# Mix features of two heads taken together, on alternating row halves of the array

## The reference, cut to what matters

```python
q = (hidden_states @ Wq.T).reshape(b, s, H, HD)
k = (hidden_states @ Wk.T).reshape(b, s, H, HD)
v = (hidden_states @ Wv.T).reshape(b, s, H, HD)
qf = jax.nn.elu(q @ Wf.T) + 1.0
kf = jax.nn.elu(k @ Wf.T) + 1.0
kv = jnp.einsum('bshf,bshd->bhfd', kf, v)
out = jnp.einsum('bshf,bhfd->bshd', qf, kv)
k_sum = kf.sum(axis=1)
norm = jnp.einsum('bshf,bhf->bsh', qf, k_sum)[..., None] + 1e-06
out = (out / norm).reshape(b, s, D)
```

## Time and profile before

| | |
|---|---|
| median of three runs | 1080.4 us |
| the profiled execution | 1081.49 us, its span 1079.7 us |
| mean granted TensorE clock | 0.978 |
| TensorE busy | 1024.7 us, 95% |
| VectorE, ScalarE, GpSimd busy | 793.2, 637.3, 133.2 us |
| mix stage on TensorE | from 74.75 us to about 222 us |

### The profile page before, as it was taken

How to read it: one execution, slowest core, us unless ns; L and a number is a source line. 1 busy time by engine, 2 the same in 40 slices (tenths; PEclk the granted TensorE clock), 3 DMA queues, 4 the chain that set the end, 5 groups by cost and what they waited for, 6 DMA issues and landing times.

```text
span 1079.7 us, 15085 instructions
## 1 busy us (share of the span) xinstructions
PE 1024.7 (95%) x5227; PEld 878.8 (81%) x5227; DVE 793.2 (73%) x1094; ACT 637.3 (59%) x825; POOL 133.2 (12%) x185
## 2 busy tenths in 40 slices
PE   3999999999999999988989899999999999999988
PEld 3899999998788899877778787777888878787766
DVE  6347878774677868767674588888887888788687
ACT  3257776722321133577774457777777777778582
POOL 2002223230010002132211020000000000000013
PEclk9999999999999999989899899999999999999989
DMA  8652413245646664311103279999999999999986
GB/s 283 181 176 59 117 60 113 64 124 171 176 122 201 186 192 122 115 39 39 40 1 109 92 287 366 381 353 384 385 387 344 376 387 363 372 358 388 332 308 237
DMA packets 140508, 237.33 MB, mean 220 GB/s; under 512 B 6908, under 2 KB 48124, under 8 KB 137892
## 3 DMA queue, kind: packets, MB, share of 16 engines
q1 hardware_dynamic: 135780, 225.91, 61.3%
q0 software_dynamic: 1760, 6.37, 1.5%
q10 hardware_dynamic: 2912, 4.34, 1.1%
HBM read 206.56 MB, written 30.03 MB: 219 GB/s over the span
## 4 chain that ended last, share of the span: by engine, by line
PE 68%; DVE 11%; ACT 7%; issue 5%; DMA 5%; POOL 2%; SPq 1%; ACTq 0%; DVEq 0%; POOLq 0%
PE bank L1297 28%; PE bank L962 5%; PE bank L964 5%; PE bank L963 5%; DMA raw<-in_wffn 5%; PE bank L976 4%; PE bank L978 4%; PE bank L977 4%; DVE wlo L1371 2%; PE bank L1096 2%; DVE dense L1634 1%; PE bank L1284 1%; ACT a_all L860 1%; PE bank L1179 1%; PE bank L1038 1%
## 5 line engine op out<-in xcount | busy, mean ns | idle before, releaser
L1671 DVE TENSOR_TENSOR wlo<-raw,whi 128x2048 fp32r<-128x2048 f32 x72 | 164.6, 2289 | 27.9 <-ACT whi L860 27.6
L860 ACT ACTIVATE a_all<-raw 128x2048 fp32r<-128x2048 f32 x72 | 138.1, 1917 | 53.2 <-DMA raw<-in_wffn 31.7
L860 ACT ACTIVATE whi<-raw 128x2048 fp32r<-128x2048 f32 x72 | 138.0, 1917 | 44.7 <-DMA raw<-in_wffn 23.0
L1371 DVE TENSOR_TENSOR wlo<-raw,whi 128x1024 fp32r<-128x1024 f32 (+1 forms) x72 | 120.5, 1678 | 46.6 <-ACT whi L652 45.8
L652 ACT ACTIVATE whi<-raw 128x1024 fp32r<-128x1024 f32 (+1 forms) x72 | 89.0, 1241 | 97.6 <-PE bank L964 47.7
L1671 DVE TENSOR_TENSOR t_all<-raw,a_all 128x2048 fp32r<-128x2048 f32 x36 | 82.5, 2293 | 39.2 <-ACT a_all L860 38.9
L962 PE MATMUL bank<-a_all,whi 128*128 128x384 f32 x320 | 109.3, 341 | 0.0
L964 PE MATMUL bank<-a_all,wlo 128*128 128x384 f32 x320 | 107.9, 337 | 0.0
L963 PE MATMUL bank<-a_all,whi 128*128 128x384 f32 x320 | 107.6, 336 | 0.0
L1297 PE MATMUL bank<-a_all,xg 128*128 128x512 f32 x360 | 106.8, 411 | 0.0
L1297 PE MATMUL bank<-whi,t_all 128*128 128x512 f32 x288 | 100.3, 410 | 0.0
(11 more groups left out here) (277 smaller groups left out, 2112.7 us busy)
## 6 DMA issues: line engine op xcount, KB each, us to landing
raw<-in_wffn SPq DMA_DIRECT2D x144, 512.0 KB
raw<-in_wffn SPq DMA_DIRECT2D x72, 1024.0 KB
raw<-in_wall SPq DMA_DIRECT2D x28, 1024.0 KB
raw<-in_wall SPq DMA_DIRECT2D x32, 512.0 KB
yrows<-zero SPq DMA_DIRECT2D x24, 512.0 KB, 7.0
y_rows<-zero SPq DMA_DIRECT2D x8, 1024.0 KB, 8.6
dense<-yrows SPq DMA_DIRECT2D x8, 512.0 KB, 7.7
y_rows<-dense ACTq DMA_DIRECT2D x16, 256.0 KB, 5.4
```

What stands on the lines that cost most here:

```text
L860: act.activation(hi_ring[u % RAW], raw[:, u % RAW, :], ACT.Copy).then_inc(hi_done, 2)
L1371: dve.tensor_tensor(ring(wlo, k), part(k), ring(whi, k).bitcast(F32), ALU.subtract).then_inc(lo_done, width(k))
L1671: dve.tensor_tensor(lo_ring[u % RAW], raw[:, u % RAW, :], hi_ring[u % RAW].bitcast(F32), ALU.subtract)\
```

## The change

The two heads of a chunk are taken together. In an even step the K features of heads h and h + 1 are made, in an odd step the kv of both heads, and then the Q features of both. Their matmuls alternate: head 0 of the chunk on the rows 0 to 63, head 1 on the rows 64 to 127, into different banks. The mixes of both heads stand in the next even step, one ahead of the piece and one behind it. The kv of odd heads gets its own columns of bank 0 (kv_bank). The numbers of matmuls and of operations on the other engines stay as they are.

```diff
@@ -382,12 +382,17 @@
 
         def feature(h, i):
 
+            g, part_ = i % 2, i // 2
             b = gp_bank("feat", 4 * h + i)
-            if i < 2:
-                return qf[h % 2][:, i, :], b[:, 0:N]
-            if i == 2:
-                return kf[h % 2][:, 0:2, :], b[:, :].rearrange("p (t f) -> p t f", t=2)
-            return kf[h % 2][:, 2, :], b[:, 0:FD]
+            if h % 2:
+                return qf[g][:, part_, :], b[:, 0:N]
+            if part_ == 0:
+                return kf[g][:, 0:2, :], b[:, :].rearrange("p (t f) -> p t f", t=2)
+            return kf[g][:, 2, :], b[:, 0:FD]
+
+        def kv_bank(g):
+
+            return bank[0][:, 2 * P * (g % 2):2 * P * (g % 2) + 2 * (HD + 1)]
 
         block = ctx.enter_context(nc.Block())
...
-                b = bank[0][:, 0:2 * (HD + 1)].rearrange("p (f d) -> p f d", f=2)
-                act.wait_ge(kv_full, g + 1)
+                b = kv_bank(g).rearrange("p (f d) -> p f d", f=2)
+                act.wait_ge(kv_full, g // 2 * 2 + 2)
...
 
-                if h >= 2:
-
+                if h >= 2 and h % 2 == 0:
+                    act.wait_ge(kv_full, h)
+                elif h >= 3:
                     act.wait_ge(qf_lo, h - 1)
-                    act.wait_ge(kv_full, h - 1)
...
-                act.wait_ge(feat_done, 4 * h + 2)
-                if h >= 2:
-                    act.wait_ge(mix_full, h - 1)
-                act.activation(qf_s[h % 2][:, 0, :, :], qf[h % 2], ACT.Copy).then_inc(qf_hi, 1)
+                if h % 2:
+                    act.wait_ge(feat_done, h + 1)
+                    if h >= 3:
+                        act.wait_ge(mix_full, h - 1)
+                    for g in range(2):
...
-                if 1 <= h <= H:
+                if h % 2 and h < H:
                     kv_high(h - 1)
+                    kv_high(h)
...
+            def mix(g):
+
+                pe.wait_ge(kv_ready, g + 1)
+                if g >= 1:
...
             for h in range(H + 2):
                 k = PAIRS + 2 + h
-                if h >= 2:
-                    g = h - 2
...
+                if h >= 2 and h % 2 == 0:
+                    mix(h - 2)
...
-                if 1 <= h <= H:
-                    g = h - 1
-                    pe.wait_ge(feat_done, 4 * g + 4)
-                    if g >= 1:
...
+                if h >= 2 and h % 2 == 0:
+                    mix(h - 1)
+                if h % 2 and h < H:
+                    pe.wait_ge(feat_done, h)
+                    if h >= 3:
+                        pe.wait_ge(kv_ready, h - 1)
+                    for g in (h - 1, h):
+                        for f in range(2):
+                            for t in range(NT):
+                                last = pe.matmul(kv_bank(g)[:, f * (HD + 1):(f + 1) * (HD + 1)], kf[g % 2][:, t, f * P:(f + 1) * P],
+                                                 v_tok[:, t, g, :], start=(t == 0), stop=(t == NT - 1))
+                        last.then_inc(kv_full, 1)
...
                 if h < H:
-                    for i in range(4):
-                        gp_take(pe, "feat", 4 * h + i)
...
-                            if i < 2:
-                                last = pe.matmul(b[:, 0:N], w[:, w_part, i * P:(i + 1) * P], q[:, x_part, :], start=(n == 0), stop=(n == 2))
-                        for t in range(0, 2) if i == 2 else range(2, 3) if i == 3 else ():
+                    for i in (0, 2):
+                        b = []
+                        for g in range(2):
+                            gp_take(pe, "feat", 4 * h + i + g)
+                            b.append(gp_bank("feat", 4 * h + i + g))
+                        rows_ = [slice(0, HD), slice(HD, P)]
+                        if h % 2:
+                            f = slice(i // 2 * P, i // 2 * P + P)
                             for n, (x_part, w_part) in enumerate(((0, 0), (0, 1), (1, 0))):
-                                last = pe.matmul(b[:, (t % 2) * FD:(t % 2 + 1) * FD], kk[:, x_part, t * P:(t + 1) * P],
-                                                 w[:, w_part, :], start=(n == 0), stop=(n == 2))
-                        last.then_inc(gp_full, 1)
+                                for g in range(2):
+                                    last = pe.matmul(b[g][:, 0:N], wf_s[rows_[g], w_part, f], qk[h // 2 % 2][rows_[g], 0, x_part, :],
+                                                     start=(n == 0), stop=(n == 2))
+                                    if n == 2:
+                                        last.then_inc(gp_full, 1)
+                        else:
+                            for t in range(0, 2) if i == 0 else range(2, 3):
+                                for n, (x_part, w_part) in enumerate(((0, 0), (0, 1), (1, 0))):
+                                    for g in range(2):
+                                        last = pe.matmul(b[g][:, (t % 2) * FD:(t % 2 + 1) * FD], qk[h // 2 % 2][rows_[g], 1, x_part, t * P:(t + 1) * P],
+                                                         wf_s[rows_[g], w_part, :], start=(n == 0), stop=(n == 2))
+                                        if n == 2 and t > 0:
+                                            last.then_inc(gp_full, 1)
...
+                if h >= 2 and h % 2 == 0:
+                    mix_out(h - 2)
...
+                if h >= 2 and h % 2 == 0:
+                    mix_out(h - 1)
+                for g in (h - 1, h) if h % 2 and h < H else ():
...
+                    b = kv_bank(g).rearrange("p (f d) -> p f d", f=2)
+                    dve.wait_ge(kv_hi, h + 1)
...
-                        if i == 1 or i == 3:
+                        if i == 3:
                             dve.wait_ge(gp_dve, gp_by[:gp["feat", 4 * h + i] + 1].count("dve"))
-                            dve.sem_inc(feat_done, 2)
+                            dve.sem_inc(feat_done, 1)
```

More of the change, by code:

```diff
@@ L1027, in _ @@
             pe.wait_ge(bo_added, 1)
+            def mix(g):
+                pe.wait_ge(kv_ready, g + 1)
+                if g >= 1:
+                    pe.wait_ge(mix_done, g)
+                pe.wait_ge(qf_lo, g + 1)
+                for n, (kv_part, q_part) in enumerate(((0, 0), (0, 1), (1, 0))):
+                    for f in range(2):
+                        last = pe.matmul(bank[1][:, 0:N], kv[g % 2][:, kv_part, f, :], qf_s[g % 2][:, q_part, f, :],
+                                         start=(n == 0 and f == 0), stop=(n == 2 and f == 1))
+                last.then_inc(mix_full, 1)
             for h in range(H + 2):
                 k = PAIRS + 2 + h
-                if h >= 2:
-                    g = h - 2
-                    pe.wait_ge(kv_ready, g + 1)
-                    if g >= 1:
[L1034 to L1040, removed]
+                if h >= 2 and h % 2 == 0:
+                    mix(h - 2)
                 if k < T_V:
@@ L1451, in _, with mix_out @@
             qk_low(0, 1)
+            def mix_out(g):
+                own, other = (slice(HD * (p % 2), HD * (p % 2) + HD) for p in (g, g + 1))
+                o = bank[1]
+                dve.wait_ge(mix_full, g + 1)
+                if g >= 4:
+                    dve.wait_ge(mix_norm, (g - 4) // 2 + 1)
+                dve.tensor_scalar(norm[own, g // 2 % 2, :], o[other, 0:N], 1e-6, None, ALU.add).then_inc(norm_ready, 1)
+                dve.tensor_copy(moT[own, g // 2, :], o[own, 0:N]).then_inc(mix_done, 1)
             def invert(c, half):
@@ L1463, in _ @@
                     lo(n)
-                if h >= 2:
-                    g = h - 2
-                    own, other = (slice(HD * (p % 2), HD * (p % 2) + HD) for p in (g, g + 1))
-                    o = bank[1]
-                    dve.wait_ge(mix_full, g + 1)
-                    if g >= 4:
-                        dve.wait_ge(mix_norm, (g - 4) // 2 + 1)
-                    dve.tensor_scalar(norm[own, g // 2 % 2, :], o[other, 0:N], 1e-6, None, ALU.add).then_inc(norm_ready, 1)
-                    dve.tensor_copy(moT[own, g // 2, :], o[own, 0:N]).then_inc(mix_done, 1)
+                if h >= 2 and h % 2 == 0:
+                    mix_out(h - 2)
                 if k < T_V:
                     qk_low(h // 2 + 1, h % 2)
-                if 1 <= h <= H:
-                    g = h - 1
+                if h >= 2 and h % 2 == 0:
+                    mix_out(h - 1)
+                for g in (h - 1, h) if h % 2 and h < H else ():
                     own, other = (slice(HD * (p % 2), HD * (p % 2) + HD) for p in (g, g + 1))
-                    b = bank[0][:, 0:2 * (HD + 1)].rearrange("p (f d) -> p f d", f=2)
-                    dve.wait_ge(kv_hi, g + 1)
+                    b = kv_bank(g).rearrange("p (f d) -> p f d", f=2)
+                    dve.wait_ge(kv_hi, h + 1)
                     dve.tensor_tensor(kv[g % 2][:, 1, :, own], b[:, :, 0:HD], kv[g % 2][:, 0, :, own].bitcast(F32), ALU.subtract)
```

7 lines of the change are left out of this document (2 added, 5 removed).

## The result

The changed kernel takes 1128.1 us (median of 4 runs, 1126.24 to 1131.53) against 1077.5 us for the kernel before (4 runs): the ratio is 1.047, with a 95% interval of 1.0415 to 1.0523, so it is slower by 4.7%. The prediction was 1141 us, in a range of 1120 to 1162. The direction and the mechanism came as predicted; one term of the sum, the pitch of the alternating matmuls, was mis-sized, and the drain was priced rightly for a reason that doesn't hold.

A forecast was written before the change was run, and what follows sets the result against it. TensorE was taken to bound the kernel, so new waits ahead of the mixes count in full: 1081.5 us + 44 (stage) + 16 (low clock) = 1141.5, forecast as 1141 us, range 1120 to 1162.

The forecast's parts named there:

- the sum: Whole kernel: 1081.5 us plus 44 for the longer mix stage plus 16 for the low clock, 1141.5.
- the pitch of the alternating matmuls: Q and K features on TensorE: one start every 0.114 us for both shapes, a floor taken from the kv matmuls.
- the drain: TensorE changing between 128-row and 64-row matmuls: none seen, priced at nothing; at most 5 us in all.
- What bounds the stage: Mix stage: TensorE, busy 73.41 of 74 us, so a microsecond of new wait is a microsecond of span.
- The chain from the Q features to the mix: Odd step into next mix: 7.35 us from first Relu through ScalarE, VectorE and GpSimd, with TensorE waiting eight times.
- rival 2: Q and K features: the row halves overlap fully, stage +37 us before the clock, 1134 us; chance 0.20.
- The clock: TensorE behind each of eight waits: granted clock falls, losing 2.2 us each, less 1.6 already paid; +16 us.
- The cover of the K features: Even step: K chain of about 6.0 us hidden by 2.05 + 4.16 of TensorE work; 1.1 late at the first pair.
- The other side: Mix stage: overlap hides the second half's matmuls and the mix does not wait, 1062 us; chance 0.02 for faster.

The follow-up runs named there:

- The filled wait: Changed kernel plus 60 TensorE matmuls that nobody reads, behind the Q features of each odd step; 1117.4 us, 1.038 of the kernel before.
- The kernel with the other orders: Changed kernel with mixes one step later, VectorE reading the first mix sooner, ScalarE splitting weights before copies, last mix behind last piece; 1058.9 us, 0.983.
- the later mix alone: Changed kernel with only its mixes moved one step later, behind the piece and behind the kv of odd steps; 1079.7 us, 1.0047 of the kernel before.

## Why the prediction was right, and where it was wrong

- **What bounds the stage: right.** TensorE had no slack, so a new wait in its order was paid in full, less only what the overlap saved.
- **The chain from the Q features to the mix: right**, 7.40 us for 7.35, eight waits, in the predicted place, and nothing later gave the time back. Copying one head earlier took 1.0 us off each wait.
- **The pitch of the alternating matmuls: wrong.** "I take 0.114 for both shapes" rested on the kv matmuls, which use all 128 rows and follow one another. That floor does not hold across two halves: eighteen K matmuls took 1.25 us to the next start, 0.069 each. In the single starts two partners begin 0.003 us apart, and the pairs follow at 0.11 to 0.12 us, as single matmuls did before. The first Relu starts 0.89 us behind the first Q matmul (156.11 less 155.22), 1.02 with a pitch of 0.114. This is rival 2, full overlap, +37 in place of +44 before the clock. The rule of the Trainium skill ("TensorE: Matmul & The Clock Gate", Part 3, "Measured speedup vs the span model"), that distinct row groups run concurrently, agrees: two halves gain 1.8 times (twice 1.14 us for nine matmuls, over 1.25). The prediction had set it below a floor taken from rows of the other kind.
- **The clock: right in size.** Mix and piece at full clock take 5.30 us; behind the eight waits they took 16.4 us more in all, 2.05 on average (1.4 to 2.7) for the 2.2 predicted. The filled wait gives 16.3 from the stage as a whole. The price per wait was worked from rows of other places and held.
- **The drain: the sum right, the reading wrong.** Each change between 128-row and 64-row matmuls does cost some 0.2 us, in both kernels. The rows above show it: the piece behind the K features starts at 173.91, and its second matmul 0.28 us later, where the third follows at 0.17. In the single starts the first of the new kind also comes 0.20 us behind the last K or kv matmul, where those follow at 0.11; from mix to piece, both of 128 rows, neither is seen. The prediction's check took its pitch from the same stretch, gap included, so it could not find one. The earlier trace rows show it too: six Q features take 1.15 us and six matmuls of the mix 1.14, but six of a piece 1.04 (4.16 over 24). The sum was spared because a pair of heads has four such changes before and four after.
- **The cover of the K features: right.** No wait stands ahead of the kv, except 1.0 us at the first pair (1.1 predicted).
- **The sum.** By rival 2 the stage should grow by 37 plus 17.6, some 55; it grew by 54.5. By the forecast it was 61.6, 7.1 too much, and the pitch alone is 7 of it. The other 7 us between 1141.5 and the profiled 1127.24 lie outside the stage, where the code is unchanged. Ahead of it are 4.0: the kernel before ran its first weights at a pitch of 0.43 until 27.93, the changed one at 0.23 from 21.47 on. In the experiments, whose beginning is also unchanged, the first features started anywhere from 70.26 to 73.08. Behind the stage 4.8 are gone, of which 1.6 was predicted (the low clock of the earlier trace rows). The rest is not an effect of the change that these runs can show.
- **The other side.** The prediction said that the gain needs an order in which the chain fits into what TensorE has in between, and priced it at 1062. The kernel with the other orders has that order and gave 1058.9, or by its ratio 0.983 of 1080.4, 1062. Getting there also took VectorE's order, which the prediction did not speak of: the later mix alone gave 1079.7.

## What to carry to other kernels

A saving on the bounding engine counts only if that engine has work while the results go round the other engines. When two steps are fused, follow the chain from each result to its first reader, and put a piece of other work at least as long between them. Then look at the in-order engines that read the results: work for later data ahead of a read of the shared bank is the next wait. And an idle gap of the matmul engine can have a second price behind it, here 2.05 us on average for a gap of 7, and 1.3 to 1.6 us for one of 1.25, in five cases of eight.

## What the runs showed of the hardware

- Matmuls of 64 rows on different halves cost little more than half each, their weight loads included: 12 of 384 columns in 1.32 us, 18 of 256 columns in 1.31, where 6 and 9 on one half took 1.31 and 1.21.
- They need not alternate: blocks of 3 overlap fully (1.33), blocks of 6 and 9 in part (1.78, 2.03). TensorE starts the idle half's matmul before earlier ones of the busy half, with three of these still to start. So for row halves the order of the starts is not the order of the program.
- A change between 128-row and 64-row matmuls cost some 0.2 us, 0.09 ahead of the first matmul and 0.11 behind it.
- Behind an idle time of 1.25 us the clock fell in five cases of eight, and not in three, with the same work around it. Behind one of 7 us it fell in eight of eight, and the low clock cost 1.4 to 2.7 us.
